# A small column copy in a selective-scan kernel, moved from GpSimd to VectorE

## What is computed

```
def step(state, inp):
    d_t, b_t, c_t, u_t = inp
    dA = jnp.exp(d_t[..., None] * A)
    state = dA * state + (d_t * u_t)[..., None] * b_t[:, None, :]
    y_t = jnp.einsum('bdn,bn->bd', state, c_t)
    return (state, y_t)
```

## Time and profile before

| | us |
|---|---|
| median of 3 runs | 1458.35 |
| lowest and highest | 1455.82, 1458.52 |
| the profiled execution, its own time | 1456.31 |
| its span, first to last instruction | 1454.5 |

### The profile page before, as it was taken

One profiled execution on the slowest core, in us unless ns is written; L12 is line 12 of the kernel. 1 busy time (PEld: TensorE's weight loads), 2 busy tenths in 40 slices (PEclk: granted clock), 3 DMA queues, 4 the chain that ended last, 5 costly groups with the idle time before them and its releaser, 6 DMA issues.

```text
span 1454.5 us, 23554 instructions
## 1 busy us (share of the span) xinstructions
PE 1379.5 (95%) x8652; PEld 1076.8 (74%) x8652; DVE 1026.0 (71%) x1377; ACT 889.0 (61%) x1461; POOL 904.2 (62%) x578
## 2 busy tenths in 40 slices
PE   7999999999999999988899999999999999999887
PEld 4445469999999999456667767777767768768777
DVE  7755542332322323589899998999999998998996
ACT  4211121111111111399999989999999999999893
POOL 4222211232222222159989989989999989999995
PEclk9999999999999999989999999999999999999999
DMA  9921146766766764123342452533534443523532
GB/s 299 404 91 40 58 136 227 269 251 233 267 248 249 273 241 151 41 55 79 88 102 74 98 119 61 131 88 94 125 80 96 102 102 88 129 76 84 134 91 69
DMA packets 57761, 205.17 MB, mean 141 GB/s; under 512 B 6575, under 2 KB 32815, under 8 KB 48822
## 3 DMA queue, kind: packets, MB, share of 16 engines
q1 hardware_dynamic: 42358, 146.55, 28.9%
q0 software_dynamic: 15296, 57.19, 17.3%
HBM read 141.78 MB, written 31.00 MB: 119 GB/s over the span
## 4 chain that ended last, share of the span: by engine, by line
PE 49%; POOL 21%; DVE 10%; ACT 10%; issue 7%; DMA 3%; SPq 0%; POOLq 0%; DVEq 0%; ACTq 0%
PE bank L1518 17%; POOL hst L690 16%; PE bank L1531 8%; PE bank L1463 7%; DVE hst L1363 5%; ACT dA L883 4%; PE bank L1723 3%; PE bank L1703 3%; POOL dbuT L672 3%; ACT dbuT L872 2%; DMA hst<-hst 2%; PE bank L1585 2%; POOL xpad L650 1%; PE bank L1493 1%; PE bank L1592 1%
## 5 line engine op out<-in xcount | busy, mean ns | idle before, releaser
L1363 DVE TENSOR_TENSOR_SCAN hst<-dA,carry,bank 128x512 f32<-128x512 f32 x512 | 631.4, 1266 | 52.4 <-PE bank L1703 41.2
L690 POOL TENSOR_TENSOR hst<-hst,c_bc 128x2048 f32<-128x2048 f32 x127 | 581.8, 4592 | 20.9 <-DVE hst L1363 6.0
L1703 PEld LDWEIGHTS bank<-ident,dbuT 128*128 128x128 f32 x2048 | 241.7, 142 | 180.1 <-issue 93.0
L883 ACT ACTIVATE dA<-delta,negA 128x512 f32<-128x512 f32 x512 | 357.2, 714 | 5.9 <-DVE hst L1363 5.8
L1703 PE MATMUL bank<-ident,dbuT 128*128 128x128 f32 x2048 | 316.3, 278 | 41.0 <-DVE hst L1363 35.9
L872 ACT ACTIVATE dbuT<-duT,bT 128x512 f32<-128x512 f32 x382 | 271.8, 712 | 8.1 <-PE bank L1703 8.0
L1518 PEld LDWEIGHTS bank<-f_sb,w_gu 128*128 128x128 f32 x2240 | 255.5, 192 | 2.7 <-ACT f_sb L754 1.0
L1518 PE MATMUL bank<-f_sb,w_gu 128*128 128x128 f32 x2240 | 256.0, 275 | 0.7 <-ACT f_sb L754 0.7
L1723 PE MATMUL bank<-ident,hst 128*128 128x128 f32 x1520 | 215.7, 273 | 3.4 <-DMA hst<-hst 3.4
L625 POOL TENSOR_TENSOR x_sb<-x_sb,neg_half 128x1 f32<-128x1 f32 x35 | 23.0, 656 | 260.5 <-DVE x_sb L1180 260.5
L1723 PEld LDWEIGHTS bank<-ident,hst 128*128 128x128 f32 x1520 | 176.2, 142 | 4.2 <-DMA hst<-hst 4.1
(11 more groups left out here) (212 smaller groups left out, 1760.6 us busy)
## 6 DMA issues: line engine op xcount, KB each, us to landing
w_gu<-in_w_gu SPq DMA_DIRECT2D x35, 2048.0 KB, 7.3
c_bc<-c_rows SPq DMA_DIRECT2D x64, 512.0 KB, 4.2
hst<-hst POOLq DMA_DIRECT2D x31, 1024.0 KB, 9.1
sorted_x<-sg_a SPq DMA_DIRECT2D x12, 387.0 KB, 11.4
x_sb<-sorted_x SPq DMA_DIRECT2D x35, 129.0 KB, 7.2
x_sb<-in_x SPq DMA_DIRECT2D x8, 512.0 KB, 7.7
w_d<-in_w_d SPq DMA_DIRECT2D x1, 4096.0 KB, 21.3
x_mix<-x_sb SPq DMA_DIRECT2D x1, 4096.0 KB, 31.5
```

The lines of the kernel that those rows point to most:

```text
L690: pool.tensor_tensor(h[:], h[:], c, ALU.mult).then_inc(hc_ready, 1)
L883: act.activation(dA[:, at % DA_BUFS, :], delta[q % B][:, d, :], ACT.Exp, scale=negA[:, d, n:n + 1]).then_inc(dA_ready, 1)
L1363: v.tensor_tensor_scan(h[:, d, :], dA[:, at % DA_BUFS, :], bank[4 + u % 2][:], carry1[q % B][:, n, d:d + 1], ALU.mult, ALU.add).then_inc(s ...
L1703: ins = pe.transpose(bank[4 + u % 2][:, i * P:(i + 1) * P], dbuT[(DS * q + n) % DBU_BUFS][:, i, d * P:(d + 1) * P], ident[:])
```

## The change

VectorE makes the copy in place of GpSimd. It stands before the second scan of the next state index: `CARRY_AT = 1` is the place of that scan within its four. GpSimd's multiplication waits until the copy is done, which it now learns from VectorE.

```
@@
+CARRY_AT = 1
@@ GpSimd
                     pool.wait_ge(scan_done, unit(q, DB * n + DB))
                     if q < CHUNKS - B:
-                        pool.tensor_copy(carry1[q % B][:, n, :], h[:, :, CH - 1]).then_inc(carry_done, 1)
+                        pool.wait_ge(carry_done, g + 1)
                     pool.wait_ge(c_loaded[n // 2 % 2], 64 * q + 16 * (n // 4 + 1))
-                    if q < CHUNKS - B:
-                        pool.wait_ge(carry_done, g + 1)
                     c = c_bc[:, n % C_BUFS, :].unsqueeze(1).broadcast_to([P, DB, CH])
@@ VectorE
+            def keep_carry(g):
+                q, n = divmod(g, DS)
+                v.wait_ge(scan_done, DB * g + DB)
+                v.tensor_copy(carry1[q % B][:, n, :], hst[g % STATE_BUFS][:, :, CH - 1]).then_inc(carry_done, 1)
@@ VectorE, in the loop over the units of chunk q
                 for u in range(UNITS):
+                    if u % DB == CARRY_AT and (q or u > DB) and DS * q + u // DB <= DS * (CHUNKS - B):
+                        keep_carry(DS * q + u // DB - 1)
```

## The result

The changed kernel takes **1481.38 us** (median of 4 runs, 1480.09 to 1484.26), the kernel before, run beside it, 1458.43. The ratio is 1.0164 [1.0152, 1.0177], so the change costs about 23 us. The forecast was 1485 in a range of 1459 to 1505.

The account below looks back on a forecast made before the run. TensorE and VectorE were taken to hand the pace back and forth. Held copies 4.3 plus copies themselves 0.8 gave 5.1 us per chunk, 25.5 for chunks 1 to 5, plus 1.5 in chunk 0: +27, forecast 1485, range 1459 to 1505.

Parts of the forecast that it names:

- GpSimd's copies, worth nothing: Taking 96 copies of 0.33 us each off GpSimd gains nothing on the path that sets the end.
- The copy itself, 0.8 us per chunk: On VectorE each added copy costs about 0.1 us; about half of 16 per chunk are hidden, leaving 0.8 us.
- The put-off multiplication, nothing: GpSimd's multiplication waits for VectorE's copy, starting 1.6 us later at state index 3; slack covers it, priced at nothing.
- The copy beside GpSimd's work, 4.3 us per chunk: VectorE's copy stands still until GpSimd's streaming instruction is over, costing 4.3 us per chunk.
- Copy(5): VectorE's copy for state index 5 waits 2.0 us for GpSimd's multiplication; idle time takes most, 0.3 us taken.
- Copy(7): VectorE's copy for state index 7, due at 992.2 beside GpSimd's multiplication and four pieces; 0.4 us taken.
- the dear bound: If VectorE cannot get in between GpSimd's pieces, 4 to 5 us per chunk come on top: +50, or 1508.
- Copy(9): VectorE's copy for state index 9 meets a just-begun GpSimd multiplication and waits about 3.9 us; 2.1 us taken.
- Chunk 0, 1.5 us: VectorE's 4.01 us wait for a merge hides what comes before it, except a merge start up to 1 later; 1.5 taken.
- Rival 1: VectorE's copy is not held up and only its own length counts: +4.4 us, or 1463; chance 0.25.
- Rival 2: GpSimd's relief shortens VectorE's merge wait in chunk 0 by 3.3 us, making the kernel faster, about 1455; chance 0.06.
- Rival 3: Every VectorE copy waits until GpSimd has nothing left but the waiting multiplication, unhidden: over 1508; chance 0.04.

Follow-up runs that it names:

- the kernel with reductions: The changed kernel with all 96 VectorE column copies written as a sum over one element (tensor_reduce), same place and waits: 1458.03 us, ratio to before 1.0008.
- The spare reductions: The kernel before plus 96 additional one-element reductions on VectorE at the change's places, results unused, GpSimd's copies kept: 1459.85 us, ratio 1.0019.
- The gate alone: The kernel before, GpSimd still copying, but its copy and multiplication start one scan later in chunks 0 to 5: 1468.69 us, ratio 1.0083.
- the one-element copy: The kernel before plus 96 additional 128x1 copies on VectorE at the change's places, results unused: 1459.02 us, ratio 1.0014.
- taking away the hold of index 7: The changed kernel with the copy of state index 7 alone written as a one-element reduction: 1492.88 us, ratio to the kernel before 1.0256.
- the spare kernel: The kernel before plus 96 additional 128x4 copies on VectorE at the change's places, results unused, GpSimd's own work kept: 1742.49 us, ratio 1.1965.
- the kernel with six reductions: The changed kernel with the copies of state indices 5, 7, 8, 9, 10 and 11 written as reductions: 1475.68 us, ratio to before 1.0131.

## Why the prediction was right, and where its sizes were off

**The bound.** TensorE and VectorE hand the pace back and forth, and a late VectorE passes on: right. The two waits swapped their sizes, and no other wait of these two engines grew by as much, apart from that of the same transposes' weight loads, which goes with it (32.9 us to 43.0). The next is TensorE's for `make_delta`, 4.2 us. GpSimd's own waits ahead of the multiplication grew more, from 13.0 us (copy included) to 43.6, but the kernel with reductions has 34.3 of them and loses nothing.

**GpSimd's copies, worth nothing.** Right as the kernel stood (1457.01 without them). Within the change the relief is not idle: it offsets the put-off multiplication.

**The copy itself, 0.8 us per chunk.** The mechanism is right, the size too large: I had about 4 us in all. The spare reductions, with nothing else changed, cost 2.7 between the medians; in their profile chunks 2 to 4 are 0.4 us longer than before and chunks 0, 1 and 5 are not longer. The kernel with reductions is alike (102.79 in chunk 3 where before has 102.35), and its median is 0.9 above before.

**The put-off multiplication, nothing.** The sum is right, its reason wrong. The gate alone costs about 12 us; I said that the relief comes "only some five indices on" and then dropped both. Together they come to nothing, which the price was right about for a reason that I did not have.

**The copy beside GpSimd's work, 4.3 us per chunk.** This was the term that decides, and it is the one that is shown: with reductions in the same place 23.4 us are gone, and the measured term is 3.5 per chunk in chunks 2 to 5. The Trainium skill, in "VectorE: DVE Perf Modes", section "Mode 2×_2P — use both read ports for one tensor", had float32 copies between SBUF tensors use both ports, and in "SBUF — State Buffer", section "SBUF: two separate sides", the shared pair is an exclusive lock. The runs agree: the four-element copy is held (3.27 us in the median beside an unhindered GpSimd), the one-element copy and the reduction are not (0.13). On one point they go further: where GpSimd's instructions overlap, the hold did not end with the instruction that the copy met, but up to five boundaries on. Against the single terms:

- Copy(4), 0.1 taken: 0.14 long, not held, since it came due at the very end of mul(3).
- Copy(5), hold 2.0 forecast, 1.9 measured; 0.3 taken for the path, 1.28 felt and 0.72 left at index 7. The idle 0.59 and 0.70 hid less than I let them.
- Copy(7), 0.4 taken, 1.15 measured. It did not get in between the pieces, which I had named as the dear bound.
- Copy(8), 0.4 taken, nothing measured. It met the boundary between `make_du` and the pieces.
- Copy(9), hold 3.9 forecast, 2.4 measured, 2.1 taken, 1.54 measured. The copy came due 59.0 us into the chunk where I had 58.1, the multiplication began at 57.0 where I had 57.4. The hold is GpSimd's remainder, so a second of lag in either engine moves it one for one.
- Copies 10 and 11, 0.5 each: 0.67 and nothing, and 0.54 given back at index 13.

Too little at 5 and 7 and too much at 8 and 9 nearly cancel.

**Chunk 0, 1.5 us.** 5.6 measured. The same two scans in the kernel with reductions:

```profile
706.56 3.61 DVE L1369 TENSOR_TENSOR_SCAN hst<-dA,carry,bank 128x512 f32<-128x512 f32 x3
...
713.75 1.28 DVE L1369 TENSOR_TENSOR_SCAN hst<-dA,carry,bank 128x512 f32<-128x512 f32 x1 [3.58 <-PE bank L1709]
```

Ahead of the stall the changed kernel is 7.2 us later (713.74 against 706.56), behind it 5.8 (719.56 against 713.75). The stall gave back 1.4 us. I had it hide what comes before it, all but about 1.5. I had taken its end to hang on the merge alone. The merge's issue moved by only 1.25 us (704.13 to 705.38), and yet the end of the stall moved with VectorE. It is TensorE's transpose that ends it, in order behind others that had waited for VectorE's scans. Whether the merge's transfer came in between is not shown by these rows. TensorE's clock has a part as well. It stood at 0.50 in 703.4 to 706.6, behind a wait of 3.14 us that the held copy(9) had brought, and by unit 45 the changed kernel had fallen back by another 0.9 us while no long copy was due. It stood at 0.50 again in 717.1 to 720.3, ahead of the end of the stall (in the kernel with reductions in 712.4 to 715.7; before, neither).

In all: 5 x 3.5 + 0.5 more in chunk 1 + 5.6 = 23.6 from holds, where I had 5 x 4.3 + 1.5 = 23, and about 1 where I had 4. That the total came within 4 us is in part luck: the chunks from 1 on were priced too high by 1.1 us each and chunk 0 too low by 4, and single holds missed either way. The prediction also had nothing of TensorE's clock, which shows in the changed kernel's time in chunk 0 alone, but makes up most of what taking away the hold of index 7 cost. Its lower bound is 1475 where it is worked out and 1472 where its range is given, without a reason.

**The rivals.** Rival 1, not held, is refuted by the rows; the kernel with reductions is what it would have looked like, at 1458.03 where I gave 1463. Rival 2's relief exists and is used up by the gate. Rival 3, each copy held for GpSimd's whole run, did not come: where GpSimd's instructions follow end to end a copy is let in at the next boundary, in the spare kernel all 96. That kernel's 1742 us come from every copy meeting a GpSimd instruction, since there no multiplication waits for it. In the overlapping rows the rival is true for as long as the row lasts.

**The signs.** Copies with a short median, each held one ending with a GpSimd instruction, none long at 0 to 3, chunk 6 as before (99.99 us against 99.98), mul(3) later against its chunk by 1.7 (23.52 us after the second scan of index 1 where it was 21.81): as named. Chunks 1 to 5 are 4 us longer, not 5; no copy is longer than 2.57; and TensorE's wait for the scans grew by 9 us in four chunks, less than I said.

## What to carry to other kernels

A tiny instruction is not priced by its length but by what it may have to wait for. Before moving one to VectorE, look at what GpSimd runs at that moment, and whether the form of the instruction (a copy of several float32 elements between SBUF tensors, here) is one that waits. If it is, write it in a form that doesn't, a sum over one element here, before moving anything. And price collisions as one schedule, not as a list: in this kernel, removing one held copy cost 11 us, of which 7.5 came through TensorE's clock, which had fallen behind the stall. So when a stall costs more than its length, look at the granted clock of the stretch behind it.

## What the runs showed of the hardware

- A VectorE copy of 128x4 float32, SBUF to SBUF, ends 0.02 to 0.04 us after GpSimd's running instruction, whatever is left of it, up to 4.35 us. The same transfer as a reduction takes 0.13 to 0.16, and a copy of 128x1 0.13.
- 96 such copies on VectorE beside an unhindered GpSimd cost 285 us, for 287 us of holds, with TensorE's granted clock at 0.91 in that stage.
- After TensorE had waited 2.15 us for VectorE, its granted clock was 0.50 for some 3.4 us in chunks 1, 3 and 5 of the kernel with six reductions and 1.00 in chunk 2, and the same instructions took 1.85 us in place of 1.12. The chunks with the fall were 1.5 to 1.7 us longer.
- Where GpSimd's instructions follow each other end to end (0.01 to 0.06 us of overlap in the records), VectorE gets in between two; where they overlap by 0.18 to 0.36 us (multiplications 4.8 long in place of 4.55, `make_du` 1.5 in place of 1.28, pieces 0.95 in place of 0.69) it does not, over up to five boundaries. A wait of GpSimd ends the overlapping in nearly every case. That the issue of a transfer starts it is what all the traces have in common; no run tested it by itself.
